# Loading x behind the edge gathers in the first stage of a graph and expert kernel

## The chip, the cores and the metric

The kernel runs on one core of one Trainium2 chip. The metric is the device time of one execution in microseconds. Before the change the median of three runs is 2069.12 us (2066.21 to 2073.44).

## What is computed

The input x has 6250 nodes of 256 numbers, and 206,250 edges sorted by destination. A normalised x goes through one graph layer and a mixture of eight experts, both added to x. The kernel's first layer is the first of two graph convolutions:

```
_layernorm(x):  (x - mean) / sqrt(var + 1e-5)           # per node
_gcn_conv(x, W, b):
    h    = x @ W
    dinv = rsqrt(number of edges that end in a node + 1)
    out  = segment_sum(h[src] * dinv[src] * dinv[dst], dst) + b
h = relu(gcn_conv(layernorm(x), W1, b1));  h = relu(gcn_conv(h, W2, b2))
x = x + h
x = x + mixture(layernorm(x))      # top 2 of 8 experts, 256 -> 1024 -> 256
```

The change touches the first convolution only, up to the point where its adjacency counts are summed.

## The kernel before

**The blocks.** The nodes lie in 49 blocks of 128. Everything around the change is in `build_layer_one` (L315 to L1079), where each engine has a program in a fixed order and waits on semaphores. The first half of it prepares; the second half (`together`) walks through steps n, one "bank" of ten destination nodes per step.

**The preparation.** The bounds of the edges of each bank are found in five columns (`COLS`). For a column c, VectorE and ScalarE find where its edges begin (`refine(c)`, L647 and L984), GpSimd issues five edge gathers (L544 to L548, semaphore `got[c]`), VectorE makes lane and code tables of them (`table(c)`, L666), TensorE turns them (`turn(c)`, L835), ScalarE copies the turned tables out (L1031), VectorE marks them (`compare(c)`, L688), and TensorE counts (`count_below`). In VectorE's list at L694 to L720 the seven groups of x stand between these (`loads(g)`, L597: it waits for one group of seven blocks and takes the statistics of each block). After the last `compare` come 49 aggregations of the statistics (L723), the degrees and their roots, and from these the scale of every row (`scale_in`).

**The products.** TensorE also multiplies each block of x with the weights: `XW_FIRST` (17) products before the first turn, `XW_EACH` (4) before each of the four others, so 33 in the preparation. ScalarE keeps the result in x's place (`keep`, L1000), and waits for the block's statistics before it, since the product overwrites x. The other `LATE` (16) products come one per step in `together` (`weigh_late`, L900).

**The steps.** `rows_at(n)` (L232) gives the rows that become ready in step n: the kept ones spread over the `LATE` steps, and one late product. ScalarE writes the upper half of a row (L1071) after it has emptied bank n (L1055); VectorE writes the lower half two steps later (`lows`, L736). Before that, in every third step, VectorE builds the one-hot tables of three banks (L802). TensorE computes bank n, then the late product of the step, then a part of the sum of block 0 (`sum_part(0, ...)`, six parts in steps `FIRST_AT` = 14 to 19, some eight 128x512 products each).

**The stores.** The queue of SyncE loads x at L490 to L495: group 0 at once, the other six after the first `refine`. In `together` (L501) it stores the seven groups of finished rows in order, group g when the lower halves of all its seven rows are there (L504), and only behind the seventh the counts of block 0 (`adj`, L511). ScalarE can't empty the first bank of block 2 into the same buffer before that store has landed (L1052). From step 28 on GpSimd gathers finished rows (`take`, L562).

Of the kernel before, what the change touches and what calls it, by code (L numbers as in the profile page):

```python
# [69 lines left out]
BANK_ITEMS = 5  # L70
SPAN = BANK_ITEMS * STEP
BANKS_ALL = NODES // SPAN
COLS = -(-BANKS_ALL // P)
# [22 lines left out]
BANKS_D = DENSE * P // SPAN  # L96
COLS_D = BANKS_D // P
LAST = [(P * (b + 1) - 1) // SPAN for b in range(DENSE)]
FIRST_AT, FIRST_PARTS = 14, 6
assert FIRST_AT > LAST[0] + 1 and FIRST_AT + FIRST_PARTS < LAST[1] + BANKS  # L100
LAG_SUM, SUM_PARTS = 2, 10
LAG_COMBINE, LAG_HIGH, LAG_LOW = 12, 15, 28
XT_BLOCKS, XT_RING = 2, 4
XT_LOADS = -(-BLOCKS // XT_BLOCKS)
XW_FIRST, XW_EACH = 17, 4
XW_LAST = XW_FIRST + (COLS - 1) * XW_EACH
LATE = BLOCKS - XW_LAST
LOW_LATER = 2
# [81 lines left out]
def bc(ap, shape):  # L190
    return ap.to_broadcast(shape)
# [109 lines left out]
def choose(k, eng, together=None, apart=None):  # L301

    if eng.engine not in k.fits_flag:
        flag = eng.alloc_register("fits_flag")
        eng.load([flag], k.fits[0:1, 0:1])
        k.fits_flag[eng.engine] = eng.snap(flag, min_val=0, max_val=1)
    with eng.If(k.fits_flag[eng.engine] > 0):
        if together:
            together()
    with eng.Else():  # L310
        if apart:
            apart()


def build_layer_one(k, gst):  # L315
# [17 lines left out]
    with ExitStack() as st:  # L333
# [102 lines left out]
        got = [sem(f"m_got{c}") for c in range(COLS)]  # L436
# [21 lines left out]
        def load_turned(eng, g):  # L458

            n = min(XT_BLOCKS, BLOCKS - g * XT_BLOCKS) * P  # L460
            o = g * XT_BLOCKS * P
            eng.dma_start(x_t[:, g % XT_RING, :, 0:n],
                          k.io["x_turned"][:, o:o + n].rearrange("(c p) n -> p c n", p=P)).then_inc(xt_in[g % XT_RING], 16)
# [5 lines left out]
        def at_lag(n, lag):  # L469

            return [b for b in ENDED if DONE[b] + lag == n]

        def copies(c):

            return 2 * len(FOLDS) * (c + 1) if c < COLS_D else 2 * len(FOLDS) * COLS_D + len(FOLDS)
# [7 lines left out]
        @block.sync  # L483
        def _(sp):
            with nc.allow_non_contiguous_dma(reason="the first edge of each tile"):
                sp.dma_start(heads, k.io["heads"][None, :].to_broadcast([P, EDGE_TILES])).then_inc(heads_in, 16)
            sp.dma_start(w[:], k.io["L0_gnn_W1"].rearrange("(c p) n -> p c n", p=P)).then_inc(w_in, 16)
            for g in range(XT_RING):
                load_turned(sp, g)
            for g in range(X_LOADS):  # L490
                n = BLOCKS // X_LOADS
                if g == 1:
                    sp.wait_ge(first_ready, 1)
                sp.dma_start(xs[:, g * n:(g + 1) * n, :],
                             k.io["x"][g * n * P:(g + 1) * n * P, :].rearrange("(b p) d -> p b d", p=P)).then_inc(x_in[g], 16)  # L495
            sp.dma_start(brow[:], k.io["L0_gnn_b1"][None, :].to_broadcast([P, D])).then_inc(b_in, 16)
            for r in range(XT_RING):
                sp.wait_ge(xt_in[r], 16 * len(range(r, XT_RING + XW_LAST // XT_BLOCKS, XT_RING)))
            sp.wait_ge(b_in, 16)

            def together():  # L501
                n = BLOCKS // X_LOADS
                for g in range(X_LOADS):
                    sp.wait_ge(lo_done, max(ROW_PLACE[r] for r in range(g * n, (g + 1) * n)) + 1)  # L504
                    sp.dma_start(k.rows_d[0][g * n * P:(g + 1) * n * P, :].rearrange("(b p) d -> p b d", p=P),
                                 k.rows[0][:, g * n:(g + 1) * n, :]).then_inc(rows0_out, 16)
                for n in range(STEPS):
                    for b in range(DENSE):
                        if LAST[b] + 1 == n:
                            sp.wait_ge(looped, b + 1)  # L510
                            sp.dma_start(k.adj[b], counts[:, b % 2].rearrange("p h d -> p (h d)")).then_inc(stored[b % 2], 16)  # L511
                    for b in at_lag(n, LAG_LOW):
                        sp.wait_ge(lo2_done, PLACE[b] + 1)
                        sp.dma_start(k.rows_d[1][b * P:(b + 1) * P, :], k.rows[1][:, b, :]).then_inc(k.rows1_out, 16)
                for q in range(2):
                    sp.wait_ge(stored[q], 16 * ((DENSE + 1 - q) // 2))
                sp.wait_ge(rows0_out, 16 * X_LOADS)
            sp.wait_ge(fits_ready, 1)
            choose(k, nc.sync, together)
# [68 lines left out]
        def _(dve):  # L588
            count = [0]

            def link(ins):

                count[0] += 1
                ins.then_inc(step, 1)
                dve.wait_ge(step, count[0])

            def loads(*gs):  # L597

                n = BLOCKS // X_LOADS
                for g in gs:  # L600
                    dve.wait_ge(x_in[g], 16)
                    for b in range(g * n, (g + 1) * n):
                        nc.vector.bn_stats(stats[:, b, :], xs[:, b, :]).then_inc(norm_ready, 1)
# [43 lines left out]
            def refine(c):  # L647

                dve.wait_ge(chunk_in[c], 16)
                for j in range(FINE_V):  # L650
                    seek = nc.vector.tensor_scalar(junk_v[:, j * CHUNK:(j + 1) * CHUNK], low(chunk[:, c, :]), aim[:, c, j:j + 1],
                                                   start_f[:, c:c + 1], ALU.is_lt, ALU.add, accum_out=first[:, c, j:j + 1])
                dve.wait_ge(fine, (BANK_ITEMS - FINE_V) * (c + 1))
                link(nc.vector.tensor_scalar(first[:, c, FINE_V:], over[:, c, :], -0.5, middle_f[:, c:c + 1], ALU.mult, ALU.add))
                nc.vector.tensor_copy(first_i[:, c, :], first[:, c, :]).then_inc(first_ready, 1)

            def turners():

                link(nc.vector.tensor_single_scalar(node_h[:], node_i[:], 7, ALU.arith_shift_right))
                nc.vector.tensor_copy(node_block[:], node_h[:])  # L660
                link(nc.vector.scalar_tensor_tensor(node_lane[:], node_h[:], -float(P), node_i[:], ALU.mult, ALU.add))
                for out, node, n in ((to_lane, node_lane, P), (in_block, node_block, COL_BLOCKS)):
                    nc.vector.tensor_tensor(out, bc(k.lane_b[:, None, 0:n], [P, SPAN, n]), bc(node[:, :, None], [P, SPAN, n]),
                                            ALU.is_equal).then_inc(turn_ready, 1)

            def table(c):  # L666

                dve.wait_ge(got[c], 16 * BANK_ITEMS)
                shape = [P, BANK_ITEMS, P]
                nc.vector.tensor_tensor(code[:, c], rows_d[:, c, :, 0:P], bc(aim[:, c, :, None], shape), ALU.subtract)  # L670
                if c:
                    dve.wait_ge(codes_ready, c)
                link(nc.vector.tensor_single_scalar(edges_h, rows_s[:, c], 7, ALU.arith_shift_right))
                if c < COLS_D:
                    nc.vector.scalar_tensor_tensor(lanes[:, c], edges_h, -float(P), rows_s[:, c], ALU.mult, ALU.add).then_inc(lanes_ready, 1)
                nc.vector.scalar_tensor_tensor(code[:, c], code[:, c], float(BLOCKS), edges_h, ALU.mult, ALU.add).then_inc(codes_ready, 1)
# [11 lines left out]
            def compare(c):  # L688

                items = slice(c * COL_ITEMS, (c + 1) * COL_ITEMS)  # L690
                dve.wait_ge(t_copied, copies(c))
                nc.vector.tensor_scalar(below[:, items], edge_cell[:, items, 0], CELLS2 - 0.5, None, ALU.is_lt).then_inc(below_ready, 1)
# [2 lines left out]
            refine(0)  # L695
            refine(1)
            turners()
            loads(1)
            refine(2)
            loads(2)  # L700
            refine(3)
            refine(4)
            table(0)
            loads(3)
            table(1)
            compare(0)
            table(2)
            compare(1)
            begin()
            loads(4)  # L710
            table(3)
            compare(2)
            table(4)
            link(nc.vector.tensor_tensor(long[:, 0:COLS * BANK_ITEMS].rearrange("p (c j) -> p c j", j=BANK_ITEMS),
                                         rows_d[:, :, :, P], aim_end[:], ALU.is_lt))
# [1900 lines left out]
```

## Time and profile before

| | |
|---|---|
| time, median of 3 runs | 2069.12 us (2066.21 to 2073.44) |
| span of the profiled execution | 2052.8 us |
| median less this span | 16.3 us |
| TensorE busy in the span | 1871.5 us (91%), mean clock 0.961 |
| VectorE, ScalarE, GpSimd busy | 66%, 36%, 56% |
| DMA over the span | mean 161 GB/s |

The span runs from the first to the last instruction of one profiled execution; its time with what lies around it isn't shown on its own, so the 16.3 us stand for that. The stage of the change is the first 126 us. A row of the trace gives start, duration, engine, line, operation, output and input with their shapes, how many instructions are taken together, and in brackets the idle time before it and what ended that.

### The profile page before, as it was taken

How to read it: one execution, taken by the hardware profiler on the slowest of the kernel's cores; microseconds unless marked ns; L12 is line 12 of the kernel's file. 1: busy time of each engine (PE TensorE's matmuls, PEld its weight loads, DVE VectorE, ACT ScalarE, POOL GpSimd, SP SyncE). 2: the span in 40 equal slices, each digit the busy share in tenths (PEclk: the TensorE clock that was granted, in tenths of full speed). 3: DMA queues.
4: the chain of work that ended last, by engine and by line, in shares of the span. 5: the costliest groups of instructions: out<-in, count | busy, mean ns of one | idle time of the engine just before them, and what ended most of it. 6: DMA issues, size and time to landing. Idle time of an engine off the chain costs nothing. (4 is left out here: it accounts for less than half of the span.)

```text
span 2052.8 us, 40739 instructions
## 1 busy us (share of the span) xinstructions
PE 1871.5 (91%) x13425; PEld 1223.2 (60%) x13426; DVE 1351.6 (66%) x3358; ACT 733.3 (36%) x1669; POOL 1143.9 (56%) x1210
## 2 busy tenths in 40 slices
PE   5789999999999975999999999944999999999997
PEld 4545555554555532544544444423989989989996
DVE  7866766676667642566675757567676676666664
ACT  5744544444444420111111111112444444444442
POOL 6236666666666614667666666302455655555553
PEclk9999999999999997999999999975999999999998
DMA  9464555554455536787877788824233332333322
GB/s 292 121 217 167 180 191 173 174 181 167 170 181 174 177 121 215 242 278 259 266 249 270 268 303 269 283 83 193 42 50 52 49 49 47 49 49 49 50 44 27
DMA packets 126419, 329.51 MB, mean 161 GB/s; under 512 B 20736, under 2 KB 80000, under 8 KB 119360
## 3 DMA queue, kind: packets, MB, share of 16 engines
q0 software_dynamic: 59072, 142.05, 26.3%
q1 hardware_dynamic: 47376, 167.36, 22.7%
q10 hardware_dynamic: 19824, 18.23, 2.8%
q8 instruction: 82, 1.34, 0.3%
q14 instruction: 65, 0.53, 0.1%
HBM read 214.10 MB, written 113.45 MB: 160 GB/s over the span
## 5 line engine op out<-in xcount | busy, mean ns | idle before, releaser
L925 PE MATMUL mp_o<-rows,m_counts 128*128 128x512 f16 x1960 | 491.0, 382 | 8.5 <-ACT m_counts L1055 8.5
L1871 PE MATMUL rp_o<-rows,r_adj 128*128 128x512 f16 x1960 | 460.2, 382 | 31.3 <-DMA r_adj<-adj 31.3
L567 POOL DMA_INDIRECT m_x_t<-rows_d,take_src x311 | 368.2, 1184 | 202.6 <-PE mp_x L938 162.8
L1798 POOL DMA_INDIRECT r_took<-rows_d,take_src x311 | 323.7, 1041 | 186.4 <-PE rp_g L1887 122.1
L1055 ACT ACTIVATE m_counts<-mp 128x490 f16<-128x490 f32 (+4 forms) x544 | 292.2, 558 | 352.4 <-PE mp L954 346.0
L1871 PEld LDWEIGHTS rp_o<-rows,r_adj 128*128 128x128 f16 x1960 | 192.8, 98 | 251.0 <-DMA r_adj<-adj 31.8
L2427 PE MATMUL fp_h<-f_xt,w 128*128 128x256 f16 x2688 | 304.8, 274 | 0.3 <-DVE f_xt L2523 0.3
L2446 PE MATMUL fp_y<-w,f_hh 128*128 x2688 | 302.4, 273 | 0.0
L925 PEld LDWEIGHTS mp_o<-rows,m_counts 128*128 128x128 f16 x1960 | 183.0, 98 | 185.1 <-issue 11.5
L2427 PEld LDWEIGHTS fp_h<-f_xt,w 128*128 x2688 | 264.0, 98 | 31.7 <-issue 0.7
L2446 PEld LDWEIGHTS fp_y<-w,f_hh 128*128 128x128 f16 x2688 | 263.0, 98 | 30.4
L954 PEld LDWEIGHTS mp<-m_oh_cell,m_oh_lane 128*128 128x128 f16 x2560 | 163.8, 98 | 140.6 <-DVE m_oh_lane L802 24.8
L954 PE MATMUL mp<-m_oh_cell,m_oh_lane 128*128 128x98 f16 x2560 | 194.2, 208 | 29.7 <-DVE m_oh_lane L802 14.5
L2499 ACT ACTIVATE f_h<-fp_h,b 128x256 f32<-128x256 f32 x448 | 188.4, 475 | 76.1 <-PE fp_h L2427 71.4
L802 DVE TENSOR_TENSOR m_oh_lane<-lane_b,m_edge_lane 128x1920 f16<-128x1920 bf16 x171 | 201.8, 1180 | 8.9 <-PE mp L954 8.7
L2363 POOL DMA_INDIRECT out_dram<-f_weighted,f_to x112 | 184.8, 1650 | 30.4 <-issue 29.5
L180 POOL TENSOR_TENSOR held_pool<-held_pool 1x1 f32<-1x1 f32 x204 | 68.7, 339 | 210.7 <-DMA out_dram<-f_weighted,f_to 165.9
L2556 DVE TENSOR_TENSOR f_hh<-f_h,f_hh 128x512 f16<-128x512 f32 x224 | 156.1, 697 | 7.7
L802 DVE TENSOR_TENSOR m_oh_cell<-m_cells,m_edge_cell 128x1470 f16<-128x1470 bf16 x171 | 159.2, 931 | 0.0
L783 DVE TENSOR_TENSOR m_take_oh<-lane_b,take_lane 128x640 f16<-128x640 bf16 (+1 forms) x63 | 31.2, 496 | 191.4 <-PE mp_x L938 191.4
L2351 POOL DMA_INDIRECT f_xg<-xn_rows,f_stage x112 | 115.0, 1027 | 33.9 <-issue 33.4
L2532 DVE SCALAR_TENSOR_TENSOR f_y<-fp_y,b 128x256 f32<-128x256 f32 x112 | 47.4, 424 | 121.5 <-PE fp_y L2446 120.1
(260 smaller groups left out, 1877.2 us busy)
## 6 DMA issues: line engine op xcount, KB each, us to landing
adj<-m_counts SPq DMA_DIRECT2D x40, 1568.0 KB, 5.9
r_adj<-adj SPq DMA_DIRECT2D x40, 800.0 KB, 5.2
r_adj<-adj SPq DMA_DIRECT2D x40, 768.0 KB, 5.2
r_raw<-in_L_ffn_W_dram POOLq DMA_DIRECT2D x16, 1024.0 KB, 8.4
w_parts<-r_parts POOLq DMA_DIRECT2D x8, 1024.0 KB, 6.7
w<-w_parts SPq DMA_DIRECT2D x4, 2048.0 KB
rows<-in_x_dram SPq DMA_DIRECT2D x7, 896.0 KB, 20.1
rows_d<-rows SPq DMA_DIRECT2D x7, 896.0 KB, 4.6
```

What stands on the lines that cost most here:

```text
L567: pool.indirect_dma_start(out=took[:, r, :], out_offset=None, in_=k.rows_d[0], in_offset=bass.IndirectOffsetOnAxis(ap=k.take_src[:, i:i + ...
L802: nc.vector.tensor_tensor(out[:, r:r + items].rearrange("p r (v t) -> p r v t", t=2), bc(row[:].rearrange("p (v t) -> p v t", t=2)[:, None ...
L925: mm = nc.tensor.matmul(ps_o[q], counts[:, q, s, :], k.rows[0][:, s, :], start=i == 0, stop=i == BLOCKS - 1)
L954: mm = nc.tensor.matmul(bank(n)[:, i * CELLS2:(i + 1) * CELLS2], oh_lane[:, slot(n) + i, :], oh_cell[:, slot(n) + i, :], start=True, stop= ...
L1055: last = nc.scalar.activation(counts[:, q, :, lo - b * P:hi - b * P].rearrange("p h (a d) -> p h a d", d=STEP), items[:, :, (lo - first_ds ...
L1798: pool.indirect_dma_start(out=took[:, r, :], out_offset=None, in_=k.rows_d[1], in_offset=bass.IndirectOffsetOnAxis(ap=k.take_src[:, i:i + ...
L1871: mm = nc.tensor.matmul(ps_o[b % 2], adj[:, m % ADJ_RING, at:at + P], rows[:, s, :], start=s == 0, stop=s == BLOCKS - 1)
L2363: pool.indirect_dma_start(out=k.io["out"], out_offset=bass.IndirectOffsetOnAxis(ap=to[:, i:i + 1], axis=0), in_=weighted[:, i % YR, :], in ...
L2427: mm = nc.tensor.matmul(ps_h[b][:, j * PAIR:(j + 1) * PAIR], w, xt[:, q, xh, c, :], start=i == 0, stop=i == 5)
L2446: mm = nc.tensor.matmul(ps_y[s][:], hh[:, q, xh, h, s * P:(s + 1) * P], w, start=i == 0, stop=i == 3 * HB - 1)
L2499: g = nc.scalar.activation(h32[:, h, :], ps_h[b][:, j * PAIR:(j + 1) * PAIR], ACT.Gelu, bias=k.b1[:, bass.ds(ex[m + 1] * HB + h, 1)], scal ...
L2556: nc.vector.tensor_tensor(hh[:, q, 1, part], h32[:, part], hh[:, q, 0, part], ALU.subtract).then_inc(h_lo, 1)
```

## The change

x's groups 1 to 5 are no longer loaded right after the first `refine`: group g is issued when the gathers of column g - 1 have landed; group 6 follows group 5. In VectorE's list the statistics of groups 1 to 4 move behind `table(0)`, `compare(0)`, `begin` and `compare(2)`. Seven products stand before the first turn, five before each of the others, 22 come late, and the sum of block 0 begins at step 18.

```diff
-FIRST_AT, FIRST_PARTS = 14, 6
+FIRST_AT, FIRST_PARTS = 18, 6
...
-XW_FIRST, XW_EACH = 17, 4
+XW_FIRST, XW_EACH = 7, 5
...
             for g in range(X_LOADS):
                 n = BLOCKS // X_LOADS
-                if g == 1:
-                    sp.wait_ge(first_ready, 1)
+                if 1 <= g <= COLS:
+                    sp.wait_ge(got[g - 1], 16 * BANK_ITEMS)
...
             turners()
-            loads(1)
             refine(2)
-            loads(2)
             refine(3)
             refine(4)
             table(0)
-            loads(3)
+            loads(1)
             table(1)
             compare(0)
+            loads(2)
             table(2)
             compare(1)
             begin()
-            loads(4)
+            loads(3)
             table(3)
             compare(2)
+            loads(4)
             table(4)
```

## Rows read from the trace of the kernel before

**Rows 1.** Stretches: start:end, length, busy of PE, PEld, DVE, ACT, POOL, clock, DMA
```profile
30.00:50.00 20.00, 16.21 (x66) 12.12 (x67) 18.88 (x46) 10.17 (x31) 15.32 (x15) 0.91 1.08 348
...
115.00:123.00 8.00, 4.66 (x55) 2.90 (x52) 7.93 (x13) 3.35 (x7) 0.00 (x0) 1.00 1.05 373
...
126.00:770.00 644.00, 605.23 (x4651) 327.38 (x4651) 416.05 (x570) 288.33 (x565) 393.12 (x350) 0.98 0.50 172
```

**Rows 2.** Timeline of TensorE at the end of the first stage
```profile
126.04 1.89 PE L925 MATMUL mp_o<-rows,m_counts 128*128 128x512 f16 x4 [6.05 <-ACT m_counts L1055]
```

**Rows 3.** Timeline of ScalarE at the same place
```profile
125.65 1.28 ACT L1055 ACTIVATE m_counts<-mp 128x196 f16<-128x196 f32 x3 [5.42 <-DMA adj<-m_counts]
```

**Rows 4.** Lines 505, 511: issue ns min/median/max, first to last start; landing
```profile
L505 SPq DMA_DIRECT2D rows_d<-rows x2: 359/1400/2441, 111.8 to 112.2; - x2
...
DMA to landing us min/median/max: 5.4/6.5/7.5
...
L511 SPq DMA_DIRECT2D adj<-m_counts x1: 1862/1862/1862, 115.4 to 115.4; - x1
...
DMA to landing us min/median/max: 10.3/10.3/10.3
```

**Rows 5.** Timeline of VectorE from the aggregations to the last lower half
```profile
71.08 3.32 DVE L723 BATCH_NORM_AGGREGATE rows<-rows 128x2 f32<-128x6 f32 x49
...
75.62 1.16 DVE L802 TENSOR_TENSOR m_oh_lane<-lane_b,m_edge_lane 128x1920 f16<-128x1920 bf16 x1 [0.16 <-issue]
...
103.04 1.14 DVE L802 TENSOR_TENSOR m_oh_lane<-lane_b,m_edge_lane 128x1920 f16<-128x1920 bf16 x1
...
108.56 1.15 DVE L802 TENSOR_TENSOR m_oh_lane<-lane_b,m_edge_lane 128x1920 f16<-128x1920 bf16 x1
...
110.46 1.27 DVE L740 SCALAR_TENSOR_TENSOR rows<-rows,m_scale_in,rows 128x256 f16<-128x256 f32 x3
...
112.04 1.15 DVE L802 TENSOR_TENSOR m_oh_lane<-lane_b,m_edge_lane 128x1920 f16<-128x1920 bf16 x1
```

**Rows 6.** Timeline of TensorE in steps 14 to 16
```profile
103.27 1.10 PE L907 MATMUL mp_o<-m_w,m_x_t 128*128 128x256 f32 x4
...
106.35 1.10 PE L907 MATMUL mp_x<-m_w,m_x_t 128*128 128x256 f32 x4
...
109.02 0.39 PE L954 MATMUL mp<-m_oh_cell,m_oh_lane 128*128 128x98 f16 x5
109.24 1.89 PE L925 MATMUL mp_o<-rows,m_counts 128*128 128x512 f16 x8
```

**Rows 7.** Timeline of GpSimd: last edge gather of column 0 and of column 4
```profile
25.02 0.95 POOL L548 DMA_INDIRECT rows<-in_edges_dram,m_first_i  x1 [0.30 <-issue]
...
51.70 0.95 POOL L548 DMA_INDIRECT rows<-in_edges_dram,m_first_i  x1 [0.30 <-issue]
```

**Rows 8.** Line 548, all 25 edge gathers
```profile
DMA to landing us min/median/max: 4.5/6.1/6.8
```

**Rows 9.** Line 494, x's seven loads, then line 505, its first store alone
```profile
DMA to landing us min/median/max: 8.3/20.1/22.8
...
DMA to landing us min/median/max: 4.2/4.2/4.2
```

**Rows 10.** Timeline of VectorE: the first table and the statistics of one group
```profile
39.35 0.82 DVE L670 TENSOR_TENSOR m_counts<-rows,m_aim 128x640 f32<-128x640 int32 x1
...
42.41 2.38 DVE L603 BATCH_NORM_STATS2 rows<-rows 128x6 f32<-128x256 f32 x7
```

**Rows 11.** Timeline of TensorE: products between the turns, and the last turn
```profile
44.45 5.30 PE L870 MATMUL mp_o<-m_w,m_x_t 128*128 128x256 f32 x16
...
52.28 3.86 PE L870 MATMUL mp_o<-m_w,m_x_t 128*128 128x256 f32 x16
...
58.43 1.97 PE L870 MATMUL mp_o<-m_w,m_x_t 128*128 128x256 f32 x8
...
68.73 0.60 PE L848 MATMUL mp_x<-ident,m_counts 128*128 128x128 f32 x4
```

## The prediction, made before the run

> **What bounds the kernel now.** I read the stretches first, then the timelines around the first place where TensorE stands still. From 126 to 770 us TensorE is busy for 605 of 644 us, at a clock of 0.98 [rows 1]: what arrives there late stays late, and the rest of the kernel follows it. So the question is when this stretch begins. It begins at 126.04 us, after TensorE has idled for 6.05 us behind ScalarE's emptying of a bank [rows 2], and ScalarE waited 5.42 us for the store of block 0's counts [rows 3]. That store was issued at 115.4 and took 10.3 us to land [rows 4]. It stands on SyncE's queue behind the seven stores of finished rows, and two of these were issued at 111.8 and 112.2, the third 2.44 us later, at 114.6, held up in the issue of the one before [rows 4]. Group 4 (rows 28 to 34) holds row 32, the last of the kept rows, and so waits for the last step although its late rows were done long before; groups 5 and 6 wait behind it. The path is therefore: preparation up to 75.62, the steps up to the last lower half at 112.04 [rows 5], then a burst of three row stores and the counts, 111.8 to 125.65, 13.85 us. In the steps VectorE is the bound: from 103.04 to 112.04 it has two pairs of one-hots and 13 lower halves, 2 x 1.90 + 13 x 0.395 = 8.9 of 9.0 us (prices below) [rows 5].
>
> **The preparation.** Before, the first table starts at 39.35 [rows 10], behind the statistics of two groups of x, though the last gather of column 0 was issued at 25.02 [rows 7] and gathers land in 4.5 to 6.8 us [rows 8], so by about 31.1. Afterwards the statistics wait for data that are requested only then. Group 1 is issued at about 31.5; its landing lies between 4.2 us (a store of the same size alone) and 8.3 us (x's first load, others beside it) [rows 9], nearest to the middle since gathers and turned x run beside it: 6.0, so 37.5. Statistics cost 2.3 us to the next start (42.41 to 44.7, 2.38 with the last one's end), a table 42.41 - 39.35 = 3.06 [rows 10]; the second turn starts at about 37.5 + 2.3 + 2.5 = 42.3. From there TensorE: four products and a turn take 58.43 - 52.28 = 6.15 us, a product 3.86 / 4 = 0.97 [rows 11], so a column of five 7.1. The last turn starts at 42.3 + 3 x 7.1 = 63.6, against 68.73 [rows 11]; the aggregations began 71.08 - 68.73 = 2.35 after it [rows 5], so they could begin at 66.0.
>
> The other chain is longer. GpSimd's gathers aren't moved: their last is issued at 51.70 [rows 7] and lands at about 57.2. Only then do groups 5 and 6 leave (0.4 us of issue each). The nearest row for such a pair is that of the two row stores issued 0.4 us apart, which landed after 5.4 and 7.5 us [rows 4]; so group 6 lands at 57.6 + 7.5 = 65.1, and with the turned x beside it 0.3 later. Statistics (2.3) and the last comparison (0.4) follow: the aggregations begin at 68.1 instead of 71.08, **3.0 us earlier**. The seven statistics in all, the five tables and the comparisons are the same instructions as before; their move costs nothing else. The bounds: with gathers at 4.5 and loads at 4.2 us it is 6.8 earlier, with 6.8 and 8.3 us 1.3 later (worked out at the rivals).
>
> **The steps.** Let s be the start of the first one-hot pair, 75.62 before. A pair costs 110.46 - 108.56 = 1.90 us, a lower half (112.04 - 110.46) / 4 = 0.395 [rows 5]. The 49 lower halves stay, but they now end in step 24 instead of 18, and pairs stand in every third step: nine instead of seven, 2 x 1.90 = 3.8 us more on VectorE. That is the least.
>
> TensorE adds to it. Before, VectorE finished step 14 at s + 27.4 (103.04), with five pairs and 36 rows behind it [rows 5]. After, step 18 ends with seven pairs and 35 rows: s + 27.4 + 3.8 - 0.4 = s + 30.8. Here TensorE begins the sum of block 0, and steps 18 to 21 hold a bank, a late product and a part of the sum. Such a step took 109.24 - 106.35 = 2.89 us [rows 6]; VectorE alone needs 2.2 rows x 0.395 + 1.90 / 3 = 1.5 for one. Before, only steps 14 and 15 held all three, and VectorE's own work covered them. Now the last rows wait for bank 22: the late product of step 18 starts 0.23 us after VectorE's step (103.27 - 103.04) [rows 5, 6], four steps take 4 x 2.89, less the 0.22 of bank 22 itself: bank 22 starts 11.6 us after step 18. From the start of bank 16 to the last lower half it was 112.04 - 109.02 = 3.02 us with three kept rows [rows 5, 6]; with two it is 2.6. So the rows end at s + 30.8 + 14.2 = s + 45.0, against 112.04 - 75.62 = 36.4: **8.6 us more**, 3.8 of it VectorE's pairs and 4.8 TensorE's sums.
>
> **The burst.** The last kept row is now row 26, in group 3 (rows 21 to 27). So four row stores instead of three leave behind the last step, with the counts after them. One more is 896 KB, 917,504 bytes; at the 373 GB/s of 115 to 123 us [rows 1] **2.5 us**. Below: 0, if the queue had slack, which the 2.44 us of issue speak against; above: 2.8.
>
> **The sum.** -3.0 + 8.6 + 2.5 = +8.1 us at 126.04. The rest is the same instructions in the same order: the idle span of TensorE before it hides nothing, as the wait's end moves, not its start. The first combination moves four steps back, to a step that VectorE reaches during that wait. The span becomes 2060.9; with the 16.3 us that the median lies above the span, 2077.2 against 2069.12.
>
> **Rivals.**
> 1. The preparation pays the rest back. Without six loads of x beside them the gathers land in 4.5 us [rows 8] and GpSimd is not held: 20 gathers at 0.95 + 0.30 us bring the last from 51.70 to 50.0 [rows 7]. It lands at 54.5; the loads at 4.2 us [rows 9] plus one more at 2.1 (7.5 - 5.4 [rows 4]) and 0.8 of issue put group 6 at 61.6 and the aggregations at 64.3, 6.8 earlier. TensorE then allows about 62.6, as the second turn starts 3.4 earlier too. The sum is +4.3: 2073.4, not slower by what can be told. It decides from aggregations before 66.2. For it speaks that the first table no longer stands behind x; against, that loads still run among the gathers, and with turned x made 348 GB/s from 30 to 50 us [rows 1]. The Trainium skill's page "DMA: Bandwidth & Descriptors", section "Queues, rings and completion order", says that each DMA engine goes round-robin between the queues that have work, so gathers share with x only while x is queued. By that rule the time is this rival's; the trace bears it out in part, since gathers still took 4.5 to 6.8 us.
> 2. x gates every column. Gathers at 6.8, loads at 8.3 us [rows 8, 9]: group 6 lands at 51.7 + 6.8 + 0.8 + 8.3 + 2.1 = 69.7, the aggregations start at 72.4, 1.3 later than before; the sum is +12.4, 2081.5. For it: TensorE, too, will idle before the first turns. From 30 to 50 us its granted clock was 0.91 in the mean, so part of it at the lower level, 1.2 GHz [rows 1]; sixteen matmuls then took 5.30 instead of 3.86 us [rows 11], 1.4 us for four products. The skill's page "TensorE: Matmul & The Clock Gate", Part 1, says that the lower clock is the state at rest, and activity lifts it; a trace with these gaps would show 1.2 GHz there, and by the rule some 1.8 us for a column of five. Against it: the loads no longer queue behind each other.
> 3. The stretch at 126 isn't tied to the rows. Then only the preparation counts, 2066.1. For it: TensorE idles there. Against it: the order of SyncE's queue.
>
> **How the numbers follow.** Forecast 0.52, rivals 0.23, 0.18, 0.07. A measurement of this kernel can tell about 0.3%, 6.2 us, from no change. Of the forecast nine tenths lie above 2075.3; with rival 2 slower comes to about 0.67. Rivals 1 and 3 and the rest give 0.29 for the same, 0.04 faster. The likeliest case alone spans 2074.5 to 2080; the range goes down to 2069 (preparation -4, VectorE's 3.8 alone, no longer burst) and up to 2083 (rival 2 with the longer burst).
>
> **What would show it.** In the changed kernel: the first table near 31; aggregations near 68; VectorE waiting for ScalarE in steps 21 to 24 while TensorE runs sums between banks; the last lower half near 117.6; four row stores leaving together, the counts landing near 134; TensorE's long idle of some 13 us. The prediction is wrong if VectorE stays full to its last lower half, if group 3 leaves early, or if the aggregations start before 65.

## The result and the profile after

The changed kernel takes 2079.89 us (median of 19 runs, 2070.05 to 2087.65), the kernel before 2072.84 (19 runs, 2066.21 to 2080.62) beside it: 1.0036 times, 95% interval 1.0024 to 1.0048, or 7.05 us more. Slower by a little over what can be told, as forecast (+8.1 us). All comparisons below leave out one execution, the profiled one with the gathers issued twice, which took 3806 us where the four others took 2093 to 2105.

The stretches of the changed kernel; the last, 644 us from TensorE's restart, answers to that of [rows 1]:

```profile
30.00:50.00 20.00, 8.12 (x22) 5.32 (x22) 14.63 (x29) 6.46 (x20) 15.24 (x16) 0.68 0.85 257
...
154.00:798.00 644.00, 604.22 (x4651) 326.90 (x4649) 415.80 (x570) 287.52 (x565) 388.64 (x350) 0.98 0.50 172
```

The long stretch is the same as before, 604.22 against 605.23 us of TensorE at clock 0.98. It only begins 27.6 us later than in [rows 2] (153.59 against 126.04). That is about four times the difference of the medians, so something in this comparison can't belong to the change. The timelines of VectorE, ScalarE, TensorE and SyncE of the changed kernel, in this order:

```profile
30.80 0.81 DVE L670 TENSOR_TENSOR m_counts<-rows,m_aim 128x640 f32<-128x640 int32 x1
...
62.63 0.49 DVE L692 TENSOR_SCALAR m_oh_cell<-m_edge_cell 128x640 f16<-128x640 bf16 x1 [15.44 <-ACT m_edge_cell L1031]
...
86.36 3.33 DVE L723 BATCH_NORM_AGGREGATE rows<-rows 128x2 f32<-128x6 f32 x49
...
90.89 1.16 DVE L802 TENSOR_TENSOR m_oh_lane<-lane_b,m_edge_lane 128x1920 f16<-128x1920 bf16 x1 [0.16 <-issue]
...
129.71 0.48 DVE L740 SCALAR_TENSOR_TENSOR rows<-rows,m_scale_in,rows 128x256 f16<-128x256 f32 x1 [2.00 <-ACT rows L1071]
...
132.59 0.48 DVE L740 SCALAR_TENSOR_TENSOR rows<-rows,m_scale_in,rows 128x256 f16<-128x256 f32 x1 [2.00 <-ACT rows L1071]
...
136.27 0.48 DVE L740 SCALAR_TENSOR_TENSOR rows<-mp_x,m_scale_in,rows 128x256 f16<-128x256 f32 x1
```

```profile
46.33 0.38 ACT L1005 ACTIVATE rows<-mp_o 128x256 f32<-128x256 f32 x1 [5.56 <-remote]
...
54.76 0.38 ACT L1005 ACTIVATE rows<-mp_o 128x256 f32<-128x256 f32 x1 [8.05 <-remote]
...
153.20 1.28 ACT L1055 ACTIVATE m_counts<-mp 128x196 f16<-128x196 f32 x3 [13.13 <-DMA adj<-m_counts]
```

```profile
125.62 1.09 PE L907 MATMUL mp_x<-m_w,m_x_t 128*128 128x256 f32 x4
126.55 1.89 PE L925 MATMUL mp_o<-rows,m_counts 128*128 128x512 f16 x8
128.28 0.39 PE L954 MATMUL mp<-m_oh_cell,m_oh_lane 128*128 128x98 f16 x5
128.50 1.09 PE L907 MATMUL mp_o<-m_w,m_x_t 128*128 128x256 f32 x4
...
153.59 1.89 PE L925 MATMUL mp_o<-rows,m_counts 128*128 128x512 f16 x4 [13.76 <-ACT m_counts L1055]
```

```profile
136.38 4.31 SPq L505 DMA_DIRECT2D rows_d<-rows  x4
140.74 2.71 SPq L511 DMA_DIRECT2D adj<-m_counts  x1
```

The chain behind the steps is the one of [rows 2 to 4]: four row stores leave at once, the counts behind them, ScalarE waits 13.13 us for that store and TensorE 13.76 for ScalarE. The first table starts at 30.80, 8.55 us earlier than in [rows 10]. But the aggregations, forecast 3.0 us earlier than in [rows 5], stand at 86.36, 15.3 us later, behind waits of 5.56 and 8.05 us on ScalarE and 15.44 on VectorE. In the first profile of before, no wait of either engine between 30 and 70 us is over 1.7 us. Whether the change makes these waits was the first question.

### The profile page after: what moved, and what is told of

It reads as the page before. It is cut to its first block and busy times, and to the rows that moved or that the text cites. A ratio compares the mean times of both kernels' runs of the same rounds, so it can differ in the third digit from the quotient of the medians.

```text
span 2073.1 us, 40727 instructions
## 1 busy us (share of the span) xinstructions
PE 1872.0 (90%) x13425; PEld 1225.3 (59%) x13426; DVE 1347.6 (65%) x3358; ACT 728.4 (35%) x1663; POOL 1141.4 (55%) x1210
## 5 line engine op out<-in xcount | busy, mean ns | idle before, releaser
L925 PE MATMUL mp_o<-rows,m_counts 128*128 128x512 f16 x1960 | 490.8, 382 | 16.7 <-ACT m_counts L1055 16.3
L954 PE MATMUL mp<-m_oh_cell,m_oh_lane 128*128 128x98 f16 x2560 | 194.2, 208 | 29.1 <-DVE m_oh_lane L802 14.5
L2499 ACT ACTIVATE f_h<-fp_h,b 128x256 f32<-128x256 f32 x448 | 183.0, 480 | 64.4 <-PE fp_h L2427 60.0
L2475 ACT ACTIVATE held_act<-ones 128x1 f32<-128x1 f32 x56 | 11.4, 203 | 316.2 <-PE fp_x L2411 306.5
```

The lines of the kernel that those rows point to most:

```text
L925: mm = nc.tensor.matmul(ps_o[q], counts[:, q, s, :], k.rows[0][:, s, :], start=i == 0, stop=i == BLOCKS - 1)
L954: mm = nc.tensor.matmul(bank(n)[:, i * CELLS2:(i + 1) * CELLS2], oh_lane[:, slot(n) + i, :], oh_cell[:, slot(n) + i, :], start=True, stop= ...
L2499: g = nc.scalar.activation(h32[:, h, :], ps_h[b][:, j * PAIR:(j + 1) * PAIR], ACT.Gelu, bias=k.b1[:, bass.ds(ex[m + 1] * HB + h, 1)], scal ...
```

## The experiments

**Both kernels once more.** Is the late preparation the change's, or was the first profile of before a quick execution?

> The kernel before, unchanged, a second profiled execution. The first has a span of 2052.8 us, its aggregations begin at 71.08 and TensorE restarts at 126.04. Theory A (the preparation varies between executions of one kernel, and the first profile caught a quick one): the span is 2062 to 2078, and the aggregations begin more than 4 us later than 71.08 or the span is longer elsewhere. Rival B (the preparation of the kernel before is fixed, and only the changed kernel's is long): aggregations at 71 +-1, restart at 126 +-1.

> The changed kernel, unchanged, a second profiled execution. The first has its aggregations at 86.36 and TensorE's restart at 153.59, with two waits of 5.6 and 8.1 us of ScalarE for TensorE's products between 41 and 55 us. Theory A (these waits come in some executions): aggregations between 68 and 80 this time, restart between 134 and 146. Rival B (they belong to the changed order): aggregations at 86 +-1.5, restart at 153 +-2. Both expect 45 to 46 us from the first one-hot pair to the last lower half, and 16 to 17 us from there to TensorE's restart.

Measured: the kernel before 2070.16 us, its span 2068.4, and its timelines of VectorE, ScalarE, TensorE and SyncE:

```profile
49.03 0.82 DVE L673 TENSOR_SCALAR m_oh_lane<-rows 128x640 int32<-128x640 int32 x1 [0.60 <-issue]
55.40 0.83 DVE L675 SCALAR_TENSOR_TENSOR rows<-m_oh_lane,rows 128x640 f32<-128x640 int32 x1 [5.55 <-remote]
...
91.59 3.32 DVE L723 BATCH_NORM_AGGREGATE rows<-rows 128x2 f32<-128x6 f32 x49
...
96.13 1.16 DVE L802 TENSOR_TENSOR m_oh_lane<-lane_b,m_edge_lane 128x1920 f16<-128x1920 bf16 x1 [0.16 <-issue]
...
132.16 0.48 DVE L740 SCALAR_TENSOR_TENSOR rows<-mp_x,m_scale_in,rows 128x256 f16<-128x256 f32 x1
```

```profile
45.53 0.38 ACT L1005 ACTIVATE rows<-mp_o 128x256 f32<-128x256 f32 x1 [8.76 <-issue]
...
54.69 0.38 ACT L1005 ACTIVATE rows<-mp_o 128x256 f32<-128x256 f32 x1 [8.78 <-remote]
```

```profile
146.39 1.89 PE L925 MATMUL mp_o<-rows,m_counts 128*128 128x512 f16 x4 [5.89 <-ACT m_counts L1055]
```

```profile
132.27 3.32 SPq L505 DMA_DIRECT2D rows_d<-rows  x3
135.63 11.58 SPq L511 DMA_DIRECT2D adj<-m_counts  x2
```

The kernel before has waits of the same kind, at about the same places in time, and its aggregations 20.5 us later than in its first profile: theory A holds for it. The changed kernel's second run had 2082.19 us, aggregations at 86.97 and the restart at 154.11, as its first: there rival B holds. So the first profile was a quick execution: its own time would be about 2054.6 (2052.8 and the 1.8 us by which 2070.16 exceeds 2068.4), and no timed run of before was under 2065.8. Why it was quick isn't known. From here the changed kernel is compared with this second profile. A kernel further down with the same preparation (the kernel before with the counts first) has its aggregations at 91.70, so the second profile is the usual one.

Like with like, the change is three terms. Preparation: 86.36 - 91.59 = -5.2. From the first one-hot pair to the last lower half: 136.75 - 90.89 = 45.9 against 132.64 - 96.13 = 36.5, so +9.4. From there to the restart: 153.59 - 136.75 = 16.8 against 13.8, so +3.1. The sum, +7.2, is the restart's (153.59 - 146.39), and the medians' 7.05. That these two agree so closely is partly luck: from the restart to the end of the span the two profiles of the changed kernel differ by 6.9 us (1919.5 and 1926.4), and that of before has 1922.0.

**TensorE's sums in the steps.** The sum of block 0 is moved out of steps 18 to 23.

```diff
-FIRST_AT, FIRST_PARTS = 18, 6
+FIRST_AT, FIRST_PARTS = 22, 6
```

> The changed kernel with the sum of block 0 in steps 22 to 27 instead of 18 to 23, so that no step holds both a part of it and a late product. The recorded working (TensorE's sums are 4.8 of the 8.6 us in the steps): from the first one-hot pair to the last lower half about 40.5 us instead of 45 to 46, VectorE without waits above 0.5 us in the steps; TensorE's restart, tied to the row stores, 4 to 5 us earlier, time 4 to 5 us below the changed kernel's, about 1.0012 of the kernel before. Rival (VectorE's pairs and late products set the steps, the sums lie beside them): 45 us stay, no change in time.

Measured: 1.001 times before (0.9999 to 1.0021). The first pair stands at 88.67, the last lower half ends at 129.88: 41.2 us instead of 45.9. So 4.7 us of the steps are TensorE's sums. The rest, 41.2 - 36.5 = 4.7, is left for the late rows: two more pairs of one-hots, 3.8, and one wait of VectorE for ScalarE early in the steps, 0.67, which the kernel before doesn't have.

**The order of the row stores.** Groups leave in the order in which they are complete.

```diff
-                for g in range(X_LOADS):
+                for g in sorted(range(X_LOADS), key=lambda g: max(ROW_PLACE[r] for r in range(g * n, (g + 1) * n))):
```

> The changed kernel with the seven row stores in the order in which the groups become complete (0, 1, 2, 4, 5, 3, 6 or the like), so that only two groups are stored after the last step. The recorded working (each group in the burst holds the counts up by 2.5 us): from the last lower half to TensorE's restart 16.5 - 5 = 11 to 12 us, time 5 us below the changed kernel's, about 1.001 of the kernel before. Rival (the counts' store itself, not the stores before it, sets the wait; or GpSimd's gathers, which need all seven groups): 16 us stay, or less, with a new wait of the same length behind it, and the time is the changed kernel's.

Measured: 1.0002 (0.9989 to 1.0015); the last lower half ends at 136.14, the restart is at 147.15, 11.0 us behind it instead of 16.8. Two row stores fewer in the burst give back 5.8 us, 2.9 each.

**The late part alone.** The kernel before with two constants changed; x is loaded as before.

```diff
-FIRST_AT, FIRST_PARTS = 14, 6
+FIRST_AT, FIRST_PARTS = 18, 6
...
-XW_FIRST, XW_EACH = 17, 4
+XW_FIRST, XW_EACH = 7, 5
```

> The late part alone: 7 products ahead, 5 between, 22 late and the sum at step 18, with x loaded and its statistics taken as before. Theory (the steps and the burst are the whole loss, and what the change gains in the preparation is gained by x's loads and statistics): aggregations where the kernel before had them in its second profile, 91.5 +-1.5; from the first one-hot pair to the last lower half 45.7 instead of 36.4, from there to TensorE's restart 16.8 instead of 13.8; restart near 158.5; ratio to before 1.006. Rival (the preparation gains by having fewer products in it, and x's move is worth nothing): aggregations near 86.5, restart near 153.5, ratio 1.0035, the same as the whole change.

Measured: 1.0044 (1.0027 to 1.0062). The timelines of VectorE and of TensorE:

```profile
85.71 3.33 DVE L723 BATCH_NORM_AGGREGATE rows<-rows 128x2 f32<-128x6 f32 x49
```

```profile
152.71 1.89 PE L925 MATMUL mp_o<-rows,m_counts 128*128 128x512 f16 x4 [13.75 <-ACT m_counts L1055]
```

My theory fell and the rival stands: without x's move the aggregations are as early as with it (85.71 against 86.36). What the change gains in the preparation comes from its products: six fewer in it, and ten fewer ahead of the first turn.

**x loaded early in the changed kernel.** SyncE's wait is the old one, VectorE's order the new one.

```diff
-                if 1 <= g <= COLS:
-                    sp.wait_ge(got[g - 1], 16 * BANK_ITEMS)
+                if g == 1:
+                    sp.wait_ge(first_ready, 1)
```

> The whole change, but SyncE loads x's groups 1 to 6 right after the first refine, as before; VectorE's order is the changed one. Theory (in the preparation TensorE's late products set the end, and when x arrives does not): aggregations 86.5 +-1.5, restart 153.5 +-2, ratio to before 1.0035. Rival 1 (the waits keep the DMA engines free for the edge gathers, and that is the gain): gathers land later, aggregations near 91, restart near 158, ratio 1.006. Rival 2 (the waits hold x back, as the prediction had it): aggregations 3 to 6 us earlier than in the change, 82, restart near 149, ratio 1.001.

Measured: 1.0035 (1.0016 to 1.0054), aggregations at 84.91, restart at 151.43: the theory's time, with an end of the preparation 1.5 us earlier than in the change, 0.1 outside what the theory allowed (85 to 88) and far from rival 2's 82 and rival 1's 91. The five new waits move nothing that can be told: the six profiles with x's loads and statistics as in the change have aggregations from 84.13 to 86.97.

**The counts ahead of the last row stores.** Nothing in the counts of block 0 needs the late rows; the store only stands behind them on SyncE's queue. The same edit in both kernels:

```diff
-                for g in range(X_LOADS):
-                    sp.wait_ge(lo_done, max(ROW_PLACE[r] for r in range(g * n, (g + 1) * n)) + 1)
+                last = lambda g: max(ROW_PLACE[r] for r in range(g * n, (g + 1) * n))
+                for i, g in enumerate(sorted(range(X_LOADS), key=last)):
+                    if i == X_LOADS - 2:
+                        sp.wait_ge(looped, 1)
+                        sp.dma_start(k.adj[0], counts[:, 0].rearrange("p h d -> p (h d)")).then_inc(stored[0], 16)
+                    sp.wait_ge(lo_done, last(g) + 1)
...
-                    for b in range(DENSE):
+                    for b in range(1, DENSE):
```

> The kernel before, but SyncE stores the finished groups in the order in which they become complete, and the counts of block 0 ahead of the last two of them. Theory (TensorE's idle time before the restart is ScalarE's wait for this store and nothing else stands behind it): the counts land before VectorE's last lower half, TensorE's idle time of 5.9 goes, from the last lower half to the first sum behind it about 8 instead of 13.8, ratio 0.997. Rival (another wait takes its place: the gathers of finished rows on GpSimd need every row store, and these leave later): idle time moves to a later place, restart at most 2 earlier, ratio 1.000 +-0.001.

> The same edit in the changed kernel. Theory: TensorE's idle time of 13.7 before the restart goes but for what its rows themselves cost; from the last lower half to the first sum behind it about 3 to 6 instead of 16.8, the change comes out 11 us earlier, ratio to before 0.998, the same as the kernel before with the edit. Rival (another wait takes its place): 7.9 of idle time as with the stores in order of completion alone, ratio 1.000.

Measured: before 0.9963 (0.9949 to 0.9977), changed 0.9944 (0.9929 to 0.9959). The changed kernel with it, SyncE's queue and TensorE:

```profile
103.62 18.41 SPq L509 DMA_DIRECT2D rows_d<-rows  x5
122.08 0.56 SPq L507 DMA_DIRECT2D adj<-m_counts  x1
134.22 0.97 SPq L509 DMA_DIRECT2D rows_d<-rows  x2
```

```profile
134.64 2.12 PE L929 MATMUL mp_o<-rows,m_counts 128*128 128x512 f16 x9 [0.43 <-DVE rows L744]
...
138.19 1.04 PE L929 MATMUL mp_o<-rows,m_counts 128*128 128x512 f16 x4 [0.53 <-ACT m_counts L1059]
```

The counts leave at 122.08, 12 us ahead of the last two groups, and the wait of 13.76 us becomes one of 0.53. From the last lower half (134.59) to the restart are 3.6 us; in the kernel before they are 8.4 (133.23 to 141.61), as its theory said. The changed kernel is then 19 us below itself (2079.89 to 2060.76, 1.0036 to 0.9944), the kernel before 6.5 below itself. With the store out of the way the late products seem to pay: 2060.76 against 2065.75, with intervals that still overlap by a little. The theory had the two equal.

**Is x's move needed in that?** This kernel differs from the last only in x's loads and statistics, which are as before.

> The kernel before with the counts' store ahead of the last two groups, 22 late products and the sum at step 18; x is loaded and its statistics taken as before. It differs from after_counts_first only in x's move. Theory (the preparation gains by the products that leave it, x's move is worth nothing): aggregations 85.5 +-1.5, restart 139 +-2, ratio to before 0.9945 +-0.0015. Rival (x's move has a part in the gain once the store no longer hides it): aggregations 2 to 5 later than in after_counts_first (87 to 90), ratio 0.996 to 0.997.

Measured: 0.9934 (0.9921 to 0.9948), 2060.21 us, aggregations at 86.33, restart at 140.18. It isn't needed. This kernel and the last are the quickest of the study, and can't be told apart. This one's interval lies just clear of that of the kernel before with the counts first (from 0.9949), so the late products most likely pay.

**Which products matter.** All 27 early products ahead of the first turn, 22 late as there.

```diff
-XW_FIRST, XW_EACH = 7, 5
+XW_FIRST, XW_EACH = 27, 0
```

> As before_counts_late22, but all 27 early products stand ahead of the first turn and none between the turns; 22 are late as there. Theory 1 (the preparation gains by the number of products in it): aggregations 85.5 +-2, ratio 0.9945. Theory 2 (only products ahead of the first turn hold the tables up, those between the turns lie beside the gathers): 20 more ahead at 0.97 to 1.3 each put the first turn at 65 and the aggregations at 95 or later, ratio 0.999 or more. Theory 3 (the products between the turns are what stalls, each behind ScalarE's keeping of the one two before it): aggregations 80 or earlier, ratio 0.992.

Measured: 0.999 (0.9981 to 1.0), the time of theory 2; theories 1 and 3 are out. With the same 27 products in the preparation as the kernel of 2060.21 us, it is 11 us slower. So their place decides and not their number alone. VectorE's first comparison waits for the first turn, which stands behind all of them:

```profile
73.42 0.49 DVE L696 TENSOR_SCALAR m_oh_cell<-m_edge_cell 128x640 f16<-128x640 bf16 x1 [18.16 <-ACT m_edge_cell L1035]
```

In this profile the aggregations stand at 91.81, not at 95 or later, and the restart at 145.56, only 5.4 us behind that of the kernel of 2060.21 us. Its execution took 2062.97 us, 8.6 below the median of this kernel's 13 runs, so where the rest of the 11 us lies isn't shown.

**The sum at step 22 once more,** now with the counts first.

> after_counts_first with the sum of block 0 at step 22 instead of 18. Theory (with the store out of the way TensorE is busy 4.5 to 5.0 of every 5 us from 120 to 155, so the order in which it does sums and banks is worth at most the 1.8 us that it idles there): from the first one-hot pair to the last lower half 41 instead of 45.1, but the ratio to before 0.9935 to 0.9945, no more than 1.8 us better. Rival (VectorE's waits in steps 21 to 24 are on the path): 4.7 us better, ratio 0.992.

Measured: 0.9953 (0.9937 to 0.9969). From the first pair to the last lower half it is 40.7 us, but the restart comes at 140.78, no earlier than with the sum at 18 (138.19). The rival's 4.7 us are refuted. The 4.7 us that VectorE loses to the sums count only while row stores stand ahead of the counts: with them there, the same move of the sum gave 1.0036 to 1.001; here it gives 0.9944 to 0.9953.

**What the late signals go with.** The 25 edge gathers a second time behind the first, into a tile idle there, in the kernel before.

```diff
...
+            for c in range(COLS):
+                for j in range(BANK_ITEMS):
+                    start = bass.IndirectOffsetOnAxis(ap=first_i[:, c, j:j + 1], axis=0)
+                    pool.indirect_dma_start(out=again[:, c, j, :], out_offset=None, in_=k.io["edges"], in_offset=start).then_inc(again_in, 16)
...
```

> The kernel before with the 25 edge gathers issued a second time behind the first 25, 96 bytes a partition into a tile that is idle there; nothing waits for them before the first finished rows are gathered at about 136. It asks what the late signals between 35 and 55 go with (VectorE waited 5.55 for its own instruction at 49, ScalarE 8.8 twice for products). Theory 1 (they go with GpSimd's gathers being issued and landing): gathers now run to about 84, waits of 3 or more without a late partner go on behind 56, aggregations at 105 or later, ratio to before 1.007 or more. Theory 2 (they end near 55 whatever GpSimd does, and go with the start, the loads of x or the clock): last such wait at 55 to 57, aggregations 91.6 +-2, ratio at most 1.002.

Measured: 1.0156 (1.0136 to 1.0176), 30 us more in the medians. The profile is of the execution of 3806 us, so only the order of its waits is read. ScalarE and GpSimd:

```profile
62.90 0.38 ACT L1012 ACTIVATE rows<-mp_o 128x256 f32<-128x256 f32 x1 [10.81 <-issue]
73.39 0.38 ACT L1012 ACTIVATE rows<-mp_o 128x256 f32<-128x256 f32 x1 [10.11 <-remote]
84.59 0.39 ACT L1012 ACTIVATE rows<-mp_o 128x256 f32<-128x256 f32 x1 [10.82 <-remote]
89.51 0.38 ACT L1012 ACTIVATE rows<-mp_o 128x256 f32<-128x256 f32 x1 [4.53 <-remote]
```

```profile
81.88 0.95 POOL L554 DMA_INDIRECT m_take_oh<-in_edges_dram,m_first_i  x1 [0.30 <-issue]
105.99 0.95 POOL L559 DMA_INDIRECT rows<-in_edges_dram,m_take_i  x1 [23.15 <-DVE m_take_i L689]
```

The waits go on until 89.51, about as long as the gathers do (the last is issued at 81.88 and has still to land), where they had ended at 55 before. GpSimd then stood idle for 23.15 us before its next gather, waiting for VectorE, so the extra ones held nothing up there by being in its queue. Theory 1 holds in its time, and its pattern is seen in this one profile; no profile of an execution near 2100 us shows it.

## Why the prediction was right, and where it wasn't

**What bounds it: right.** The restart hangs on SyncE's queue, [rows 2 to 4]. The two runs with the counts first show it: the wait goes with the store's place, in both kernels. Rival 3, a stretch that isn't tied to the rows, is out.

**The preparation: the term -3.0, measured -5.2, and not for the reason given.** The step that failed is "the other chain is longer": the last gather, the landing of x's last pair, its statistics. That chain went much as worked out. The first table came at 30.80, the last pair left at 55.63 and 56.00 (forecast 57.2 and 57.6; by the middle value of [rows 8], 6.1, these would have been 0.6 later and the term -2.4), and the one of the two whose landing the trace shows took 6.1 us, inside the bounds (4.2 to 8.3). But nothing waited for it: VectorE took the statistics of the pair only at 75.22 and 80.51, with no idle time in front of either. The aggregations followed the chain of TensorE's products and turns instead, which the prediction ended at 66.0. These statistics, and TensorE's second and last turn in the changed kernel:

```profile
75.22 2.37 DVE L603 BATCH_NORM_STATS2 rows<-rows 128x6 f32<-128x256 f32 x7
...
80.51 2.38 DVE L603 BATCH_NORM_STATS2 rows<-rows 128x6 f32<-128x256 f32 x7
```

```profile
58.84 0.63 PE L844 MATMUL mp_x<-ident,rows 128*128 128x128 f32 x2
...
84.01 0.60 PE L848 MATMUL mp_x<-ident,m_counts 128*128 128x128 f32 x4
```

The aggregations start 2.35 us behind the last turn, which is the distance in [rows 5, 11]. But that turn comes 20.4 us later than the 63.6 worked out: 16.5 of it are the second turn's (58.84, forecast 42.3), behind ScalarE's waits of 5.56 and 8.05, and 3.9 belong to the three columns after it (25.2 instead of 21.3). Two runs bear it out: with x's order undone (the late part alone) the aggregations came at 85.71, with its waits undone at 84.91. So the sign of the term was right and its reason wrong; that it came out within 2.2 us is luck.

Rivals 1 and 2 fell with that step. Rival 1 forecast earlier gathers: the last was issued at 51.37 against 51.70 [rows 7] and 50.81 in the second profile of before, so GpSimd wasn't held less. It did land as early as rival 1 had it (the load that waits for it left 4.3 us after), but x's loads set nothing. Rival 2 had x gate every column: the early load shows that it gates none. The low clock that it spoke of is there, 0.68 in 30 to 50 us against 0.91 [rows 1], which is part of the time at the lower level, with TensorE busy for 8.12 of these 20 us instead of 16.21. The Trainium skill's "TensorE: Matmul & The Clock Gate", Part 1, has the lower clock as the state at rest, and this trace agrees. But the kernel before has 0.62 there in its second profile, with TensorE busy for 6.05, so the change doesn't make it:

```profile
30.00:50.00 20.00, 6.05 (x16) 3.78 (x16) 14.03 (x36) 1.37 (x5) 15.16 (x16) 0.62 1.07 348
```

**The steps: +8.6, measured +9.4.** Nine pairs instead of seven stand in the trace, and TensorE's part was 4.8, measured 4.7. Steps 18 to 21 have the period worked out, 128.50 - 125.62 = 2.88 against 2.89 [rows 6], and VectorE waits 0.33, 2.00 and 2.00 us for ScalarE in steps 21 to 23, where 21 to 24 were forecast. VectorE's own part, 3.8, was measured as 4.7, 0.67 of it that wait for ScalarE early in the steps.

**The burst: +2.5, measured +3.1.** A store measured 2.9 us, over the 2.8 given as the upper bound, which came from no row.

**The sum: +8.1, measured +7.2 at the restart and +7.05 in the medians.** The errors of the terms, -2.2, +0.8 and +0.6, partly cancel. (The chance of slower adds up to 0.65, 0.9 x 0.52 + 0.18, not 0.67.) And the absolute time was saved by a convention rather than by knowledge: the 16.3 us "with what lies around it" are 1.8 us of that and 14.5 of a profile quicker than any timed run. Since the forecast added a difference to the median, the mistake cancelled; a time built up from that profile, 2060.9 and 1.8 us, would have been 17 us too low. The absolute marks (aggregations 68, last lower half 117.6, counts landed by 134) all missed by 18 to 19 us: by the 20.5 us that the first profile's preparation was short, less what the terms were off.

## What to carry to other kernels

Before work is moved to relieve a stage, look at what the moved work stands ahead of on an in-order queue: here a wait of 13.76 us lay behind four row stores, and storing the groups as they become complete, with the counts ahead of the last two, left 0.53 of it and turned +0.36% into -0.56%. Compare a profile's span with the timed runs before its marks are used: one that is quicker than all of them, as here, can lack waits that the usual execution has. When a change has two halves, run each alone, since the one that the change is named for may do nothing.

## What the runs showed of the hardware

While GpSimd issued its gathers, engines waited as if signals came late, with no instruction left in the trace that they waited for. This shows in all profiles here but the first of before. In the second profile of before VectorE's instruction at 49.03 ended at 49.85, and the next one, which needs only that, began 5.55 us later; in the first profile the same two stand 0.04 us apart. ScalarE, at 45.53 and 54.69, waited twice for 8.8 us for products that had ended before the wait began. They are the second of the two products in the first row below, ended by 32.46, and the one in the other row, ended by 38.95:

```profile
30.49 1.97 PE L870 MATMUL mp_o<-m_w,m_x_t 128*128 128x256 f32 x8 [0.68 <-issue]
36.91 2.04 PE L870 MATMUL mp_o<-m_w,m_x_t 128*128 128x256 f32 x4 [4.46 <-issue]
```

In the kernel before with the counts first the same wait of VectorE was 6.22 us:

```profile
53.41 0.83 DVE L679 SCALAR_TENSOR_TENSOR rows<-m_oh_lane,rows 128x640 f32<-128x640 int32 x1 [6.22 <-remote]
```

Twice the gathers cost about 30 us, and in the one profile of that kernel these waits went on some 35 us longer. What delays the signals stays open, and so does whether it is the signal or the waiting engine that is late. The first profile of before has the same gathers and no such wait, so they aren't enough by themselves, and whether it is their issue on GpSimd or their landing wasn't told apart. The quick execution of the kernel with all products ahead (2062.97 of 2062.97 to 2074.24) wasn't spared: its profile has waits of 6.70 and 8.07 us on ScalarE and 7.60 on VectorE. None of the timed runs of before, 2065.8 at the least, is as quick as the first profile.
